# An inverse transform in 64x32 instead of 128x32 tiles of TensorE, in half calls on two accumulators crossed over

## The reference

```
for i in range(nl):                                  # nl = 4
    h_ft = jnp.fft.rfft2(h)
    w_c = spec_wr[i] + 1j * spec_wi[i]
    out_modes = jnp.einsum('bixy,ioxy->boxy', h_ft[:, :, :mx, :my], w_c)   # mx = my = 16
    spec = jnp.fft.irfft2(out_modes, s=(H, W))
    conv = lax.conv_general_dilated(h, conv_w[i], (1, 1), 'SAME', dimension_numbers=dn)
    conv = conv + conv_b[i][None, :, None, None]
    h = leaky(spec + conv)
h = leaky(h @ Q1_w + Q1_b)
out = (h @ Q2_w + Q2_b)[..., 0]
```

## Time and profile before

| what | us |
|---|---|
| median of 3 runs | 1433.85 |
| lowest and highest run | 1432.02, 1447.41 |
| profiled execution, its own time | 1432.21 |
| its span, first to last instruction | 1430.4 |
| layer 0, one pair | 12.14 |
| layers 1 and 2, one pair | 17.36 |
| layer 3, one pair | 20.20 |

### The profile page before, as it was taken

How to read it: one execution, slowest core, us unless ns; L and a number is a source line. 1 busy time by engine, 2 the same in 40 slices (tenths; PEclk the granted TensorE clock), 3 DMA queues, 4 the chain that set the end, 5 groups by cost and what they waited for, 6 DMA issues and landing times. The chain is left out here.

```text
span 1430.4 us, 36199 instructions
## 1 busy us (share of the span) xinstructions
PE 1290.9 (90%) x16656; PEld 705.2 (49%) x16656; DVE 546.6 (38%) x553; ACT 497.0 (35%) x934; POOL 67.0 (5%) x122
## 2 busy tenths in 40 slices
PE   4898888899999998999999989999999982789955
PEld 2555455545444445454444454444444432469945
DVE  3655554433343332333353331101111002567775
ACT  1244444233333332233333323434334341435511
POOL 2000000000000000000000000101110110000000
PEclk8999999999999999999999999999999996879977
DMA  8444346776666665766666654455544505100000
GB/s 270 161 126 122 91 123 174 231 191 191 190 201 198 189 190 179 219 183 183 187 192 189 188 160 102 97 111 124 114 95 102 124 3 123 30 0 1 2 0 15
DMA packets 39335, 192.19 MB, mean 134 GB/s; under 512 B 16304, under 2 KB 16560, under 8 KB 17456
## 3 DMA queue, kind: packets, MB, share of 16 engines
q1 hardware_dynamic: 30224, 137.44, 37.9%
q0 software_dynamic: 8960, 52.44, 10.4%
HBM read 136.89 MB, written 52.95 MB: 133 GB/s over the span
## 5 line engine op out<-in xcount | busy, mean ns | idle before, releaser
L365 PE MATMUL psum<-halo,conv 128*64 128x512 f32 x2304 | 520.8, 600 | 0.0
L365 PEld LDWEIGHTS psum<-halo,conv 128*64 128x64 f32 x2304 | 156.4, 137 | 325.5 <-issue 299.8
L594 DVE STREAM_TRANSPOSE vt<-psum 128x1024 f32<-128x1024 f32 x64 | 127.1, 1985 | 415.9 <-PE psum L341 415.9
L500 ACT ACTIVATE x_now<-psum,conv_bias 128x512 f32<-128x512 f32 x256 | 169.7, 686 | 323.1 <-PE psum L376 307.2
L483 ACT ACTIVATE spec<-psum 32x128 f32<-32x128 f32 x384 | 150.5, 392 | 298.9 <-PE psum L294 295.0
L376 PEld LDWEIGHTS psum<-dft,vt 128*32 128x32 f32 x8192 | 215.9, 110 | 76.5 <-issue 72.0
L376 PE MATMUL psum<-dft,vt 128*32 128x128 f32 x8192 | 250.1, 274 | 1.0 <-DVE vt L594 1.0
L564 DVE STREAM_TRANSPOSE xt<-x_now 128x1024 f32<-128x1024 f32 x100 | 124.2, 1243 | 283.3 <-PE psum L282 186.2
L571 DVE STREAM_TRANSPOSE ft<-psum 128x1024 f32<-128x1024 f32 x50 | 95.1, 1902 | 12.5 <-PE psum L282 12.5
L294 PEld LDWEIGHTS psum<-dft,ft 128*64 128x64 f32 x1600 | 54.9, 141 | 62.0 <-DVE ft L571 42.8
L294 PE MATMUL psum<-dft,ft 128*64 128x64 f32 x1600 | 57.3, 226 | 27.1 <-DVE ft L571 27.1
(11 more groups left out here) (133 smaller groups left out, 778.9 us busy)
## 6 DMA issues: line engine op xcount, KB each, us to landing
activations<-x_now POOLq DMA_DIRECT2D x48, 1056.0 KB, 9.9
halo<-activations SPq DMA_DIRECT2D x192, 264.0 KB, 6.6
halo<-activations SPq DMA_DIRECT2D x192, 263.9 KB, 7.4
wspec<-in_spec SPq DMA_DIRECT2D x16, 1024.0 KB, 9.5
xcol<-in_xcol SPq DMA_DIRECT2D x16, 384.0 KB, 4.5
x_now<-in_ser SPq DMA_DIRECT2D x2, 1056.0 KB, 6.9
t_lq<-in_onehot SPq DMA_DIRECT2D x1, 2048.0 KB, 15.3
t_kr<-in_causal SPq DMA_DIRECT2D x1, 2048.0 KB, 24.0
```

Source lines behind the costliest of these rows:

```text
L365: mm(acc[u][64 * r:64 * r + 64, :], conv[:, l - 1, dy, :], rows[:, at:at + 16, 0:G], start=(dy == 0), stop=False, skip_group_check=True)
L500: copy(x_now[:, k, 16 * u:16 * u + 16, 0:G], acc[u].rearrange("p (i j) -> p i j", j=G), ACT.Prelu, bias=conv_bias[:, l:l + 1], alpha=SLOPE ...
L594: vec.transpose(vt[:, k].rearrange("p h r o -> p (h r) o").rearrange("p y o -> p o y"), turned.rearrange("p a b -> p (a b)").rearrange("p ...
```

## The change

`spectral(T, u)` becomes `spectral(T, u0, crossed)`. It uses only the 64 rows of `ix` and `vt` that matter for 64 columns of output: tiles of 64 rows and 32 columns, eight at a time. The upper row half (`il` = 0) always gives the first 64 columns of each 128, the lower the last 64. One call works on two banks at a time: not crossed, the upper row tiles write into unit u0 and the lower into u0 + 1; crossed, the other way round. After both calls both units have all their columns. There are four such calls a pair instead of four whole ones, each with 32 matmuls instead of 16. The crossed call waits on the new semaphore `s_half` for the end of the first, and it alone counts `s_acc`, by two.

The first call for units 0 and 1 stands ahead of `rows_forward` or `head_hidden`, the crossed one behind; the first for units 2 and 3 stands ahead of `columns_forward` or `head_out`, the crossed one at the end of the pair. On ScalarE `head_activate` moves ahead of evictions 0 and 1 in the last layer.

```diff
-            def spectral(T, u):
+            def spectral(T, u0, crossed):
 
                 k = T % 2
-                pe.wait_ge(s_vt, T + 1)
+                if crossed:
+                    pe.wait_ge(s_half, 2 * T + u0 // 2 + 1)
+                else:
+                    pe.wait_ge(s_vt, T + 1)
                 for ih in range(4):
-                    for r in range(2):
-                        for s in range(2):
-                            g = 64 * r + 32 * s
-                            z = mm(acc[u][g:g + 32, 128 * ih:128 * ih + 128], vt[:, k, 4 * u + ih, r, :],
-                                   ix[:, s, :], start=False, stop=True, skip_group_check=True)
-                z.then_inc(s_acc, 1)
+                    for il in range(2):
+                        u, half = u0 + (1 - il if crossed else il), slice(64 * il, 64 * il + 64)
+                        col = 128 * ih + 64 * il
+                        for r in range(2):
+                            for s in range(2):
+                                g = 64 * r + 32 * s
+                                z = mm(acc[u][g:g + 32, col:col + 64], vt[half, k, 4 * u + ih, r, :],
+                                       ix[half, s, half], start=False, stop=crossed, skip_group_check=True)
+                if crossed:
+                    z.then_inc(s_acc, 2)
+                else:
+                    z.then_inc(s_half, 1)
...
-                spectral(T, 0)
-                spectral(T, 1)
+                spectral(T, 0, False)
                 if p > 0:
                     if last:
                         pe.wait_ge(s_x, 4 * T)
                         head_hidden(p - 1)
                     else:
                         rows_forward(n)
+                    spectral(T, 0, True)
                     convolve(T, 2)
                     convolve(T, 3)
+                    spectral(T, 2, False)
                     if last:
                         head_out(p - 1)
                     else:
                         columns_forward(n)
+                else:
+                    spectral(T, 2, False)
+                    spectral(T, 0, True)
                 if p < LAST:
                     columns_back(T + 1)
-                spectral(T, 2)
-                spectral(T, 3)
+                spectral(T, 2, True)
...
+                if last and p > 0:
+                    for u in range(4):
+                        head_activate(p - 1, u)
                 evict(T, 0)
                 evict(T, 1)
                 if p > 0:
                     if last:
-                        for u in range(4):
-                            head_activate(p - 1, u)
                         head_read(p - 1)
```

More of the change, by code:

```diff
@@ L140, in build_tower @@
         s_acc = sem("s_acc")
+        s_half = sem("s_half")
         s_x = sem("s_x")
```

## The result

The changed kernel takes 1490.6 us in the median of four runs (1488.69 to 1491.8), the kernel before 1440.4 beside it (1432.02 to 1447.41): a ratio of **1.035, interval 1.028 to 1.042, slower**. The profiled executions have spans of 1488.7 and 1430.4 us; their difference of 58 us is what is explained here. (The kernel before has two times, near 1433 and near 1447; a profile at the slower one, that of e7, is longer mostly behind the tower, where a stretch of 41 us has a mean granted clock of 0.50 instead of 0.71, so stages are compared one by one, the tail apart.)

What follows compares the result with a forecast made beforehand. It took TensorE to bound layers 1 to 3, but not layer 0. Layers 1 and 2 at -43, layer 3 at -21 and layer 0 at +11 sum to -53 us, from 1432.2 profiled to a forecast of 1380, range 1364 to 1430.

Steps and rivals of the forecast that it cites:

- The pace of the new tiles: Inverse step: a round of eight 64x32 tiles takes 58.5 ns, so a half call takes 0.63 us, 0.50 before L282.
- L282's burst: At L282's start, seven matmuls and eleven weight loads on eight tiles start within 0.05 us, 7 ns apart.
- rival 1: Inverse-step starts stop at 14.7 ns: row tiles don't overlap or, second cause, issue limits; about 1478 us; chance 0.13.
- rival 4: Inverse step: rounds of eight tiles in between, 70 to 95 ns; 1395 to 1430 us; chance 0.09.
- my check for the transfers: Layers 1 and 2: transfers busy for 0.63 of a pair would be busy for 0.69; a halo wait would be wrong.
- Layer 0's chain: Layer 0: L282, crossed half, evictions, L564, L571, L294 uncovered; a pair takes 13.05 us, 0.91 slower; layer +11 us.
- The covers: Layers 1 and 2: transposes before L294 have 1.4 us of cover; the `s_half` wait is covered and costs nothing.
- Rival 3: Layer 0: the granted clock falls at two idle stretches a pair, adding 10 to 23 us; about 1400; chance 0.10.
- The rule against the change: TensorE starts never below about 25 ns: 64 inverse-step instructions take 1.6 us, not 0.47; halving columns buys nothing.

Runs made afterwards that it cites:

- e7: Kernel before, with the eight halo loads of a pair in two batches of four; 1435.5 us, ratio 1.001.
- e4: Changed kernel with the il and ih loops swapped, so a half call works on four tiles at a time; 1514.0 us, ratio 1.050.
- e10: Changed kernel with 32 columns instead of 64 in each matmul of the new calls, the other half left out; 1489.2 us, one run.
- e1: Kernel before, its order and tiles kept, each inverse-step matmul issued as two of 64 columns; 1492.0 us, ratio 1.039.
- e2: Changed kernel with each halo load cut to 132 of a partition's 2112 values from layer 1's third pair on; 1447.1 us, ratio 1.009.
- e6: Changed kernel with the eight halo loads of a pair in two batches of four; 1455.2 us, ratio 1.013.
- e13: Changed kernel's new tiles and calls in the order of the kernel before, both half calls standing together; 1478.8 us, ratio 1.031.
- e5: Changed kernel's order with the tiles of the kernel before, one whole unit on each side of the transforms; 1482.1 us, ratio 1.031.

## Why the prediction was wrong

I forecast 1380 us, faster, and gave 0.18 to slower; it was 1491. By its steps:

- **The pace of the new tiles**, the step "I take 58.5 ns", is the first that failed. Eight tiles do overlap (e4), but the 7 ns between starts hold for the first 32 matmuls only. A half call takes 0.79 us from start to next start, not 0.63. The bound from L282's burst was no bound: eight starts say nothing about sixty-four. Half the columns bring only 0.10 us of it (e10), so something that goes by the number of instructions paces the rest. This is rival 1's second cause at a milder price, some 10 ns each instead of 14.7, or about 75 ns a round: rival 4. An undisturbed pair saves 0.70 us in layers 1 and 2 instead of 1.4, and 0.62 in layer 3 instead of 1.35. By itself this would have left the forecast's sign, and the time inside the stated range: 28 x 0.70 and 14 x 0.62 are 28 us saved against about 14 lost in layer 0, which makes some 1418 us.
- **A term was missing**, and this is the step that turned the sign: "Transfers are busy for 0.63 of a pair and would be for 0.69" stands without a price, and that the instructions themselves must be fetched stands nowhere. I counted instructions as time on the array and never as bytes beside 0.63 of transfer load, though the page has `q8` as a queue of its own. With the list half as long again, TensorE runs dry while loads are queued. Layers 1 and 2 should have become 20 us shorter by their undisturbed pairs and became 37 longer: 57 us. PE's idle time in them went from 9 to 46 us, which is 37, nearly all of it stops (35.8 us to "issue"); the other 20 are busy time that should have fallen and didn't, with the granted clock at 0.50 behind the stops. e1 brings the stops without the tiles, e2 takes most of them away without shortening the list, e6 some 29 us of them. None of my rivals was this; my check for the transfers asked only whether halos land in time, which they do.
- **Layer 0's chain** was right: 13.05 us forecast, 13.20 measured, 12.14 before, and both idle stretches are there on DVE, 1.71 and 1.33 us instead of 2.1 and 1.9, since the half calls are longer. e13 gives 11.92 with the order of before, so the chain does come from the order. That the layer lost 24 us and not 11 is above all stops, 7.9 us of them, and the clock behind them: 18.18 us for its second pair, and a way into layer 1 that is 3.8 us longer.

```profile
91.75 1.15 PE L295 MATMUL psum<-dft,ft 128*64 128x64 f32 x32 [1.71 <-DVE ft L585]
...
98.76 1.09 PE L283 MATMUL psum<-xt,dft 64*32 64x512 f32 x16 [1.33 <-DVE xt L578]
```

- **The covers** held: the weight loads of the crossed calls wait on the first calls for 7.7 us in all, 31 times, but no matmul does; L295 waits for no transpose in layers 1 and 2; the halos of the changed kernel are in time.
- **Rival 3**, the clock, came true in small part. Eight pairs of layer 0 take 13.18 to 13.25 us, seven of them at a granted clock of 1.00, in spite of two idle stretches under 2 us. But in the pair from 119.25 us, with no stop on "issue" and the same two stretches, the granted clock falls, L295 takes 1.83 us instead of 1.15, and the pair 13.88; the next one takes 13.99. In e5 it falls nowhere between 51 and 272 us. That is some 1.5 us in the two pairs. The clock falls above all behind the stops, and I had given its price only for layer 0.

```profile
119.25:133.13 13.88, 10.85 (x332) 6.72 (x330) 6.22 (x4) 5.63 (x12) 0.53 (x1) 0.94 0.34 110
```

- **The rule against the change.** The start-to-start floor of about 25 ns that the Trainium skill states (TensorE: Matmul & The Clock Gate, "Wait — 56ns, not 53.3ns?") is not what this trace shows: 32 starts in 0.24 us, and about 10 ns on average over a half call. Its direction, that many narrow matmuls don't come at the speed of their columns, was right, and I gave it too little.

What stays open: why short stops remain where nothing but instructions is transferred (e2), and whether the handing out of instructions or their weight loads pace a half call behind its first 32 matmuls.

## What to carry to other kernels

Halving a matmul's columns doubles the instructions, and these have two prices that the array's time doesn't show: a rate at which they and their weight loads start once the first thirty or so are gone, and the fetching of the list, which competes with the kernel's own transfers. Look at the instruction queue's packets and at how the bulk loads are queued before making a list longer, and take no sustained rate from a burst. And before moving work between two steps, follow the chain that runs through the other engines in each stage: the same order gained 0.24 us a pair where TensorE was the bound and cost 1.3 us where a chain was.

## What the runs showed of the hardware

- Packets of instructions, 16 KB each, are held up while bulk loads are queued: none in the 7.5 us from 347.3, one in the 1.5 us behind it. TensorE stood still for 3.74 us at 0.64 transfer load over the layer. Each of the 26 stops ended 2.2 to 2.9 us after such a packet began.
- The same total of transfers in two batches instead of one took a third of the idle time away (44.8 to 28.8 us) and 35 us off the run: a stop costs more than its own length, since what follows can run at 1.2 GHz (two convolutions in 8.33 us instead of 5.37).
- On eight 64x32 tiles 32 matmuls of 64 columns start in 0.24 us, then 11 to 12 in a tenth of a us after a hesitation; with 32 columns the fast part is again 32 matmuls, and the block shrinks by 0.10 us of 0.79 only.
- A block of 32 matmul instructions costs 1.01 us where half a block of 64 costs 0.94: about 0.14 us for each block cut in two.
